# Row sums of an attention kernel: additions moved from VectorE to GpSimd, three units summed on TensorE, idle products at the start, and new planned times

## The reference

```python
def proj(Wm, bm):
    y = jnp.einsum('bld,ed->ble', x, Wm) + bm
    return y.reshape(B, L, H, dk).transpose(0, 2, 1, 3)
q, k, v = proj(Wq, bq), proj(Wk, bk), proj(Wv, bv)
scores = jnp.einsum('bhid,bhjd->bhij', q, k) / jnp.sqrt(dk)
im = jnp.arange(L) % 256
scores = jnp.where(im[:, None] >= im[None, :], scores, -1e30)
attn = jnp.einsum('bhij,bhjd->bhid', jax.nn.softmax(scores), v)
s = jnp.einsum('bld,ed->ble', merged(attn), Wo) + bo
y = jnp.clip(jnp.einsum('bsi,oi->bso', x, where(weights >= 0, 1, -1)) * scale + bias, -100, 100)
result = x0 + s * silu(y)        # x is the layer norm of x0; s and y are made from x
```

## Time and profile before

| | us |
|---|---|
| Time, median of 3 runs (lowest, highest) | 1699.39 (1696.45, 1701.87) |
| The profiled execution: its time | 1697.66 |
| Its span | 1695.8 |
| PE, DVE, ACT, POOL busy, share of the span | 95%, 73%, 71%, 68% |
| TensorE's granted clock, mean | 0.987 |

### The profile page before, as it was taken

The page is one execution under the profiler, slowest core; times in us unless marked ns, Lnnn a source line. Parts: engine busy times, 40 slices in busy tenths (PEclk is TensorE's granted clock), DMA queues, the critical chain, the costliest instruction groups (busy, mean ns, idle before and its releaser), DMA issues.

```text
span 1695.8 us, 34086 instructions
## 1 busy us (share of the span) xinstructions
PE 1603.3 (95%) x11812; PEld 681.8 (40%) x11812; DVE 1237.8 (73%) x1886; ACT 1203.0 (71%) x3057; POOL 1157.7 (68%) x1156
## 2 busy tenths in 40 slices
...
GB/s 208 119 39 69 76 45 58 99 78 89 48 55 100 91 62 52 70 106 85 42 58 76 118 72 51 56 80 105 85 43 64 97 74 64 51 64 70 50 53 50
DMA packets 182952, 125.97 MB, mean 74 GB/s; under 512 B 104734, under 2 KB 157214, under 8 KB 182332
## 3 DMA queue, kind: packets, MB, share of 16 engines
...
## 4 chain that ended last, share of the span: by engine, by line
PE 61%; DVE 13%; issue 8%; ACT 7%; POOL 6%; SPq 3%; DMA 1%; POOLq 0%; DVEq 0%; ACTq 0%
PE pJ L568 24%; PE pO L791 11%; PE pJ L772 7%; POOL acc L1296 4%; DVE mx L1145 3%; SPq L1400 3%; PE pS L745 3%; PE pJ L768 2%; PE pJ L660 2%; ACT PT L893 2%; PE pJ L664 2%; PE pJ L661 2%; ACT pS L913 2%; PE pJ L711 2%; DVE acc L1173 2%
## 5 line engine op out<-in xcount | busy, mean ns | idle before, releaser
L893 ACT ACTIVATE PT<-pJ 128x512 f32<-128x512 f32 (+1 forms) x1080 | 608.6, 577 | 345.4 <-PE pJ L772 330.7
L1296 POOL TENSOR_TENSOR acc<-acc,PT 128x512 f32<-128x512 f32 (+1 forms) x640 | 779.5, 1256 | 24.0 <-PE pO L791 23.9
L772 PE MATMUL pJ<-QK 97*128 97x512 f16 (+3 forms) x1280 | 383.7, 319 | 7.5 <-ACT acc L893 6.6
L1145 DVE TENSOR_REDUCE mx<-pS 128x3 f32<-128x1536 f32 (+3 forms) x264 | 377.0, 1439 | 0.0
L1129 DVE TENSOR_REDUCE mx<-pS 128x1 f32<-128x384 f32 (+3 forms) x330 | 207.0, 633 | 100.7 <-PE pS L728 99.2
L1141 DVE TENSOR_REDUCE mx<-pJ 128x1 f32<-128x512 f32 (+3 forms) x264 | 151.4, 584 | 175.3 <-PE pJ L745 118.4
L791 PE MATMUL pO<-PT,V 128*32 128x512 f32 (+2 forms) x2800 | 259.4, 483 | 2.6 <-ACT PT L893 2.6
L913 ACT ACTIVATE pS<-pS,a 128x128 f32<-128x128 f32 (+1 forms) x480 | 245.8, 514 | 1.2
L568 PE MATMUL pJ<-xT,wh_q 128*128 128x512 f16 x512 | 194.0, 389 | 2.2 <-DVE xT L1107 1.8
L568 PE MATMUL pJ<-xT,wh_k 128*128 128x512 f16 x512 | 193.7, 381 | 2.0 <-DVE U L1240 2.0
L568 PE MATMUL pJ<-wh_v,xT 128*128 128x512 f16 x512 | 190.1, 380 | 1.3 <-DVE sg L1117 1.3
...
## 6 DMA issues: line engine op xcount, KB each, us to landing
...
QK<-aT SPq DMA_DIRECT2D x256, 1.0 KB, 1.7
...
```

The lines of the kernel that those rows point to most:

```text
L772: ins = e.matmul(slot[:, to:to + 512 - q0], k4[0:97, j, kc], q4[0:97, j, q0:512], start=True, stop=True)
L893: e.activation(probabilities_at(i), bank("t", i)[:, 0:cols], ACT.Exp, scale=SS).then_inc(s_p, 1)
L1145: e.tensor_reduce(mx[:, par, part, :].rearrange("p (j q) -> p j q", q=4)[:, 0:3, qi], pS[:, :, c0:c0 + w], AX.X, ALU.max).then_inc(s_m0, 1)
L1296: e.tensor_tensor(a, a, PT[:, RING_AT[i] % NPT, 0:width * len(heads)].rearrange("p (j q) -> p j q", j=len(heads)), ALU.add).then_inc(s_ap, 1)
```

## The change

- All additions of probabilities go to POOL; DVE's `additions` is gone, and with it the semaphore `s_av`.
- For three units, TensorE sums late key blocks itself (`DIRECT`, `direct_sums`): unit 2 (the first half of group 1) key blocks 0 to 3, units 61 and 63 (the second halves of the last two groups) key blocks 4 to 7. Each key block is multiplied by ones into the bank of the sums, four products a block, put ahead of that pair's PV. The bank is held from the first of them on. Unit 2 then needs no additions and no product of sums; units 61 and 63 keep 12 additions each (key blocks 1 to 3), whose sum is multiplied by ones on top.
- `keep_busy` has 36 idle products at the start, 8 ahead of the first q product, 5 ahead of the first v product, and 2, 3, 2 later in the first groups; 8 stand ahead of the fourth transpose of x and 3 ahead of the eighth. In all 67 instead of 36.
- The numbers of `TM` are set anew. The table itself isn't shown, but for the lines below: most entries move by under 0.3 of a tile, some by several tiles.

```diff
...
-    "o9": (-20.91, -12.08, -5.1, 0.01, -0.49, 0.43, 1.24, -16.95),
...
-    "sm": (3.81, -1.21),
...
+    "o9": (-21.11, -16.16, -6.15, 4.88, -1.0, -0.52, 0.29, -17.9),
...
+    "sm": (2.88, -1.21, -0.25, 4.18),
...
-    "add": (2.82, 4.38),
...
+    "add": (2.82,),
...
-def by_vector(kb):
-    return kb >= 6
-
-
-ADD_P = [i for i in RING if T_TILES[i][0] in ADDED and not by_vector(T_TILES[i][1])]
-ADD_V = [i for i in RING if T_TILES[i][0] in ADDED and by_vector(T_TILES[i][1])]
+DIRECT = {2: (0, 1, 2, 3), NU - 3: (4, 5, 6, 7), NU - 1: (4, 5, 6, 7)}
+
+
+def direct(n, kb):
+
+    return kb in DIRECT.get(n, ())
+
+
+ADD_P = [i for i in RING if T_TILES[i][0] in ADDED and not direct(*T_TILES[i][:2])]
 RING_AT = {i: k for k, i in enumerate(RING)}
 ADD_P_AT = {i: k for k, i in enumerate(ADD_P)}
-ADD_V_AT = {i: k for k, i in enumerate(ADD_V)}
-ADDS_P, ADDS_V = [0] * NU, [0] * NU
+ADDS_P = [0] * NU
 for _i in ADD_P:
     ADDS_P[T_TILES[_i][0]] += 1
...
+def at_bank(n):
+
+    return at_pv(n, DIRECT[n][0] & ~1) - 0.02 if n in DIRECT else at_sums(n)
+
+
 def at_sums(n):
 
     if n == NU - 1:
-        return at_pv(n, 7) + 1.17
+        return max(at_pv(n, 7) + TM["sm"][2], at_pv(n, 7) - 0.02 + 0.004)
+    if n == NU - 3:
+        return max(at_pv(n, 7) + TM["sm"][3], at_pv(n, 7) - 0.02 + 0.004)
+    if not ADDS_P[n]:
+        return at_pv(n, DIRECT[n][-1])
     return at_pv(n, 3) + TM["sm"][0] if n % NQS == 0 else at_pv(n + 1, 1) + TM["sm"][1]
...
-USES = sorted([(at_t(i), ("t", i)) for i in range(len(T_TILES))] + [(at_sums(n), ("sm", n)) for n in ADDED] +
+USES = sorted([(at_t(i), ("t", i)) for i in range(len(T_TILES))] + [(at_bank(n), ("sm", n)) for n in ADDED] +
...
+BUSY = (-200, 36), (at("qk", 0, 0) - 0.01, 8), (at("v", 0, 0) - 0.01, 5), (-45.5, 2), (-40.55, 3), (-16.75, 2)
+BUSY_X = {3: 8, 7: 3}
...
+                        for _ in range(BUSY_X.get(t, 0)):
+                            e.matmul(pO[:, :].rearrange("p (a c) -> p a c", a=4), row32[:, :],
+                                     row32[:, :].rearrange("p (a c) -> p a c", a=1).broadcast_to([P, 4, P]), start=True, stop=True)
...
-                for when, count in ((-200, 30), (at("x", 0, 3) + 0.1, 6)):
+                for when, count in BUSY:
...
+            def direct_sums():
+                for n in DIRECT:
+                    for kb in DIRECT[n]:
+                        yield at_pv(n, kb & ~1) - 0.02 + 0.01 * (kb & 1)
+                        first, last = T_FIRST[n, kb], T_LAST[n, kb]
+                        width, heads = T_TILES[first][2], len(T_TILES[first][3])
+                        ln.wait_ge(s_p, last + 1)
+                        ln.wait_ge(*bank_free("sm", n))
+                        ln.wait_ge(s_k, 3)
+                        for j in range(4):
+                            i, k = first + j // heads, j % heads
+                            probs = probabilities_at(i)[:, k * width:k * width + width]
+                            ins = e.matmul(bank("sm", n)[32 * j:32 * j + 32, 512 - width:512], ones[:, :], probs,
+                                           start=kb == DIRECT[n][0], stop=not ADDS_P[n] and kb == DIRECT[n][-1])
+                        if not ADDS_P[n] and kb == DIRECT[n][-1]:
+                            ins.then_inc(s_sm, 1)
             def row_sums():
                 for n in ADDED:
+                    if not ADDS_P[n]:
+                        continue
                     yield at("sm", n)
-                    ln.wait_ge(s_av, adds_v(n))
                     ln.wait_ge(s_ap, adds_p(n))
                     ln.wait_ge(*bank_free("sm", n))
                     ln.wait_ge(s_k, 3)
                     for j in range(4):
                         ins = e.matmul(bank("sm", n)[32 * j:32 * j + 32, :], ones[:, :], sums_of(n)[:, j, :],
-                                       start=True, stop=True)
+                                       start=n not in DIRECT, stop=True)
...
                         if i0 in ADD_P_AT:
                             ln.wait_ge(s_ap, ADD_P_AT[i0] + 1)
-                        elif i0 in ADD_V_AT:
-                            ln.wait_ge(s_av, ADD_V_AT[i0] + 1)
...
-            def additions():
-                for k, i in enumerate(ADD_V):
-                    n, kb, width, heads = T_TILES[i]
-                    yield at_t(i) + TM["add"][1]
-                    a = sums_of(n)[:, heads[0]:heads[-1] + 1, 512 - width:512]
-                    ln.wait_ge(s_p, i + 1)
-                    ln.wait_ge(s_ap, adds_p(n))
-                    ln.wait_ge(s_av, k)
-                    ln.wait_ge(s_pv, units(n) + 1)
-                    e.tensor_tensor(a, a, PT[:, RING_AT[i] % NPT, 0:width * len(heads)].rearrange(
-                        "p (j q) -> p j q", j=len(heads)), ALU.add).then_inc(s_av, 1)
...
```

More of the change, by code:

```diff
@@ L39 @@
 TM = {
-    "s": ((23.47, 26.38, 14.67, 19.02, 27.78, 32.28, 35.58), (21.14, 23.45, 28.17, 18.35, 32.83, 30.39, 35.65), (20.26, 18.31, 23.42, 26.84, 35.88, 29.2, 34.54), (20.03, 17.99, 22.49, 26.86, 35.91, 33.81, 29.82)),
-    "s0": (15.83, 19.15, 24.97, 21.26, 29.44, 34.63, 38.19),
-    "e": ((-11.45, -7.49, -2.55), (8.61, 13.37, 10.76)),
-    "held": (1.13, 0.19, 1.16, 1.94, 2.01, 1.11, 1.81, 0.56),
[12 rows of a table removed]
-    "gate": (-1.2, -0.68, 6.05, 3.79, 5.69),
-    "ln": ((-48.2, -23.74, -21.33, 35.29), (-79.63, 3.12, 7.37, 26.89), (-13.99, 0.37, -8.68, 7.42)),
-    "mx": (0.55, 0.01, -0.22),
-    "sh": (3.41, 1.96),
-    "c": ((0.78, 0.97), (-0.06, 1.16), (0.81, 0.94), (-1.08, 1.16)),
+    "s": ((23.47, 19.19, 14.67, 25.97, 27.78, 32.28, 35.49), (21.14, 23.62, 27.8, 18.53, 32.83, 30.34, 35.56), (26.84, 18.48, 23.42, 20.26, 35.88, 29.2, 34.45), (20.03, 18.16, 22.49, 26.86, 35.91, 34.17, 29.73)),
+    "s0": (18.87, 15.83, 24.28, 21.26, 29.57, 34.63, 37.34),
+    "e": ((-11.39, -7.49, -2.54), (8.61, 12.43, 10.75)),
+    "held": (1.29, 0.24, 1.3, 2.08, 1.93, 1.24, 1.94, 0.62),
[12 rows of a table added]
+    "gate": (-1.41, -0.66, 6.27, 3.81, 5.71),
+    "ln": ((-46.75, -23.74, -21.76, 35.69), (-79.63, 9.97, 7.64, 26.89), (-14.62, 0.37, -6.61, 7.42)),
+    "mx": (0.66, 0.17, -0.12),
+    "sh": (2.93, 1.96),
+    "c": ((0.77, 0.97), (-0.06, 1.16), (0.81, 0.94), (-1.08, 1.16)),
     "ex": (0.45, 1.14),
-    "mv": (2.03,),
-    "stage": (-0.82, 0.09),
-    "hl": (-6.3, 0.01),
+    "mv": (2.06,),
+    "stage": (-0.82, 0.28),
+    "hl": (-6.39, -0.01),
     "pr": (-0.09,),
-    "add": (2.82, 4.38),
-    "nrm": (-0.49, 0.77, 0.09, -0.83),
-    "out": (1.73, 3.94, 2.43),
-    "hi": ((3.5, 5.91), (2.95, 8.3)),
-    "vst": (0.51,),
+    "add": (2.82,),
+    "nrm": (-0.6, 0.81, 0.13, -1.25),
+    "out": (1.79, 3.93, 2.42),
+    "hi": ((4.17, 6.06), (2.63, 8.27)),
+    "vst": (0.43,),
     "res": (0.42, 1.37),
@@ L125, in last_batch @@
     return max(B_LAST[n, part] for part in range(n % NQS + 1))
-def by_vector(kb):
-    return kb >= 6
-ADD_P = [i for i in RING if T_TILES[i][0] in ADDED and not by_vector(T_TILES[i][1])]
-ADD_V = [i for i in RING if T_TILES[i][0] in ADDED and by_vector(T_TILES[i][1])]
+DIRECT = {2: (0, 1, 2, 3), NU - 3: (4, 5, 6, 7), NU - 1: (4, 5, 6, 7)}
+def direct(n, kb):
+    return kb in DIRECT.get(n, ())
+ADD_P = [i for i in RING if T_TILES[i][0] in ADDED and not direct(*T_TILES[i][:2])]
 RING_AT = {i: k for k, i in enumerate(RING)}
 ADD_P_AT = {i: k for k, i in enumerate(ADD_P)}
-ADD_V_AT = {i: k for k, i in enumerate(ADD_V)}
-ADDS_P, ADDS_V = [0] * NU, [0] * NU
+ADDS_P = [0] * NU
 for _i in ADD_P:
     ADDS_P[T_TILES[_i][0]] += 1
-for _i in ADD_V:
-    ADDS_V[T_TILES[_i][0]] += 1
 def added_before(tiles, k):
@@ L152, in adds_p @@
     return sum(ADDS_P[:n + 1])
-def adds_v(n):
-    return sum(ADDS_V[:n + 1])
 def units(n):
@@ L220, in wish @@
     if kind == "o" and a == B - 1:
-        return 4 * SL * B + TM["o9"][b]
+        return min(4 * SL * B + TM["o9"][b], at_sums(NU - 1) - 6.0 + 0.5 * b if b < NT // 2 else 9e9)
     if kind == "o":
@@ L263 @@
     BANK[_u], BEFORE[_u] = _k, _user[_k]
-    _until[_k], _user[_k] = max(_t, _until[_k]) + LEN.get(_u[0], 0) + HELD[_u[0]], _u
+    _until[_k], _user[_k] = max(_t, _until[_k]) + LEN.get(_u[0], 0) + HELD[_u[0]] + (at_sums(_u[1]) - at_bank(_u[1]) if _u[0] == "sm" else 99.0 if _u[:2] == ("o", B - 1) and _u[2] >= NT - 4 else 0), _u
 S_BANK, S_BEFORE = {}, {}
```

6 lines of the change are left out of this document (3 added, 3 removed), and 20 rows, old and new, of the table TM.

## The result

| | before | changed |
|---|---|---|
| Time, median (lowest, highest), us | 1697.92 (1692.04, 1701.87) | 1672.84 (1671.14, 1674.67) |
| Span of the profiled execution | 1695.8 | 1670.6 |
| Ratio of the times, 95% interval | | 0.9851, 0.9828 to 0.9875 |

The change makes the kernel 25 us faster, 1.5%. The forecast was 1681, 16 us faster: the right side, and 9 us too little.

What follows compares the result with a forecast made beforehand. PE, busy 95% of the span, was taken as the bound. From 1697.7 us, the terms -1.7 - 6.9 - 3.5 - 5.6 + 1.4 = -16.3 gave 1681, range 1667 to 1695.

Steps and rivals of the forecast that it cites:

- Start: Around the first q product: idle products in PE's gaps keep the clock full; -1.7 us, ends -2.6 and +2.
- Unit 2: At unit 2's row sums: PE's stall and half clock go, 16 products with ones come; -6.9 us, ends -9 and -2.
- The steady groups: Odd units: DVE's additions go to POOL, saving ACT's 0.47 us wait once in seven sequences; -3.5 us, ends 0 and -18.9.
- Unit 61: At unit 61's row sums: stall and half clock go, products with ones come; -5.6 us, ends -7.2 and 0.
- Unit 63: At the end: 16 products lengthen PE's list, last PV runs beside DVE's transposes; +1.4 us, ends 0 and +3.5.
- The steady gain is larger: Steady groups: half or all of DVE's 2.7 us wait a sequence reaches PE; 1669 us, chance 0.15.
- VectorE and GpSimd in each other's way: Busier POOL lengthens DVE's `L1232` and layer norm subtractions; steady term goes, 1 us more lost at start; 1685, chance 0.10.
- POOL late in each odd unit: Additions end 1.8 us later than forecast, PE waits 1 us in each of 30 units; 1711 us, chance 0.07.
- The new times: Steady order: a few products change places, layer norm later once in a sequence; 0 us, ends -5 and +5.

Runs made afterwards that it cites:

- old_idle: The changed kernel with the idle products of before (30 at the start, 6 near the fourth transpose of x): 1672.0 us, ratio to before 0.9866.
- the move alone: The kernel before with all its additions on POOL, its planned times and idle products kept, no products with ones: 1689.9 us, ratio 0.9969.
- after_old_times: The changed kernel with the old planned times, but for two numbers that the old table lacks: 1675.7 us, ratio to before 0.9883.
- no_direct2: The changed kernel with unit 2's sums by POOL's additions as before, without its products with ones: 1675.0 us, ratio to before 0.9876.
- extra_two_inputs: The changed kernel with 78 useless DVE additions of two SBUF operands, three in each odd unit from 9 to 59: 1714.7 us, ratio to before 1.0115.

## Why the prediction was right, and where it was not

The total lies in the range of 1667 to 1695 in part by luck: the steady groups gave 10.5 us more than their term, and units 2 and 61 together 3.6 less. By the prediction's own signs it was wrong in one part: the distance between equal places of two sequences was to move by at most 1 us, and moved by 2.0 (14.0 in seven). Two other signs showed in small: PE waited for POOL's additions in the steady groups, 0.3 us in each of six places, and of the 10.2 us at half clock around unit 2's row sums 3.4 stayed. Where two numbers are given below, they are from the changed kernel's two profiles, against the one of before.

- **Start, -1.7.** To unit 1's mark it was -2.1 and -2.8, but old_idle had 1.2 of it without the new idle products, so at most 0.9 to 1.6 belong to them, and that is not clear of the spread (85.80 to 87.55 among the kernels that have them). The full clock on the q product is there as forecast; in the whole time the part can't be measured.
- **Unit 2, -6.9.** Measured from mark to mark -5.3 and -4.6. The stall went; ACT's probabilities are late next (0.80 us at 129.73), and the clock is 0.93 over the 25 us around it, 3.5 us at half. Right in kind, too large by 2: the half clock did not go whole.
- **The steady groups, -3.5.** This is the step that failed. I wrote that DVE's time "lies beside PE's and is worth nothing by itself", and priced the move by what one wait in one place transmitted to ACT, seven times 0.47. Measured: -10.2 by the move alone, -14.0 with the rest. The place that I priced gave what I said: the column 5, 13, .., where DVE waited for POOL, lost 3.6 us by the move alone. The other places, which I put at nothing, gave the other 6.6. ACT had waited there for row maxima behind DVE's additions too: 17.8 us in 35 places in the whole run, of which I had read one of 0.47, and 6.1 in 14 after the move. Of the 3.8 us between -10.2 and -14.0, no part is shown to be the new order's: after_old_times, which has the old order and two stretches at half clock, spans 1405.30, and 4 us is the spread of this part. On PE the gain was in short gaps, as this one of the kernel before, behind an addition of 0.68 us that stood ahead of `U` in DVE's queue (the last line is DVE's timeline):

```profile
478.46 0.39 PE L568 MATMUL pJ<-xT,wh_k 128*128 128x512 f16 x1 [0.30 <-DVE U L1240]
...
476.65 0.68 DVE L1173 TENSOR_TENSOR acc<-acc,PT 128x512 f32<-128x512 f32 x1
```

  It stood once in each of the seven intervals of the column 9, 17, .., 2.0 us of the 3.2 that this column lost, and is gone after the move. PE's gaps above 0.15 us between units 3 and 59 sum to 44.8 us before, 39.2 with the move alone and 35.3 in the changed kernel; where the rest of the 10.2 lies on PE, the profile doesn't show. That DVE's additions were plain 0.68 us here, and that 78 plain row maxima of 0.68 us cost only 3 us with the new times, suggests that a piece of DVE's queue has no fixed price: it depends on which maxima stand behind it in that order. No run tests this by itself.
- **Unit 61, -5.6.** From 59 to 63, -3.6 and -4.0. The stall is gone, and PE is busy 26.3 us of 27 from 1605 on. Part of what is missing is clock: ahead of this place one stretch at half clock is left, which some kernels with the same order don't have (busy time by stretch, the changed kernel and old_idle).

```profile
1594.00:1601.00 7.00, 5.94 (x30) 2.06 (x34) 4.75 (x6) 2.97 (x6) 6.39 (x6) 0.76 0.05 2
1580.00:1600.00 20.00, 15.86 (x119) 5.22 (x117) 16.00 (x21) 14.55 (x33) 15.59 (x14) 1.00 0.19 42
```

  The four with the new times and unit 61's products that lack it (old_idle, no_direct2 and the two with extra instructions) take 38.07 to 38.09 us from 61 to 63, the four that have it 38.91 to 39.26: 0.8 to 1.2 us. The rest of the 5.6 is open.
- **Unit 63, +1.4.** The end is -0.2 and +1.4. The mechanism is as forecast: sums before PV, DVE's transposes beside it. (The 0.61 in the earlier trace rows is how long DVE stood idle, not the distance behind the sums' product; the sum doesn't rest on it.)
- **The rivals.** "The steady gain is larger" is what happened, by another way than the one I gave it: the places of the 2.7 us wait gave 3.6 us and the others 6.6; its 1669 is nearer to 1673 than my 1681. "VectorE and GpSimd in each other's way" is there in the durations (extra_two_inputs: 672 to 677 ns with nothing on POOL beside it, up to 1824 with), but not in the loss that it named. The layer norm's subtractions did lengthen, `L1232` (now `L1247`) got shorter, and neither is seen in the marks:

```profile
L1126 DVE TENSOR_TENSOR HL<-xs,HL 128x512 f16<-128x512 f32 x56 | 61.9, 1105 | 0.0
L1247 DVE SCALAR_TENSOR_TENSOR U<-U,Y 128x512 f32<-128x512 f32 x58 | 54.3, 936 | 16.0 <-ACT U L1001 16.0
```

  The first was 54.2 us and 967 ns a piece before, the second 61.7 and 1063. What DVE's own additions had held up of POOL, 5 us, went with them. "POOL late in each odd unit" did not come: PE's waits for POOL's additions at the row sums are 1.9 us in all, six times, none above 0.3 (the changed kernel's waits):

```profile
PE pJ L740 <- POOL acc L1311: 1.9, 6, 0.3
```

- **The new times, 0.** 3 to 5 us faster with the rest of the change, by intervals that touch, and 9 us slower without it (by the marks, 6 at units 61 and 63 and 0.5 over the steady part). The sign thus depends on the rest of the kernel.
